# Spills moved behind the loading of x, roots between relu pairs, upper count rows computed in full

## The chip, the cores and the metric

One core of a Trainium2 chip. The metric is the device time of one execution in microseconds (us); a median of several runs is taken. Engines by the profile's names: PE (TensorE matmuls; PEld its weight loads), DVE (VectorE), ACT (ScalarE), POOL (GpSimd), SP (the engine that issues the DMAs here).

## What is computed

x is 64 x 128 x 1024 (batches, times, nodes), the weight 128 x 128, gumbel one pair for each of 1024 x 1024 node pairs.

```python
h = jnp.maximum(_layernorm(x, axis=-1), 0.0)          # over the 1024 nodes
x_avg = transpose(h, (2, 0, 1)).mean(axis=1)          # over the batches
x_norm = x_avg / jnp.maximum(norm(x_avg, axis=-1), 1e-12)
sim = (x_norm @ x_norm.T + 1.0) * 0.5
adj = (sim + gumbel0 > 1.0 - sim + gumbel1)
adj_sym = jnp.clip(adj + adj.T, 0.0, 1.0)
nmask = jnp.clip(adj_sym + jnp.eye(n), 0.0, 1.0)
common = nmask @ nmask.T
struct = where(adj_sym * (common > 1) > 0, common / common.max() * common, 0.0)
W = adj * struct;  deg = W.sum(axis=0);  Wn = dinv[:, None] * W * dinv[None, :]
out = x + transpose(einsum('sd,sbt->dbt', Wn, h @ weight) + bias)
```

## The kernel before

Batches go in 32 pairs; nodes in C = 8 blocks of 128 (KC = 4 is half of it). Each engine has its own program; semaphores tie them, and the order within an engine is the order written. All DMAs are issued by SP into one queue, in order.

**Loading x** (rounds of 8 pairs, groups of two pairs, `first(r)` on PE, ACT and DVE). SP loads a pair into one of 8 slots once the relu of the pair eight back is done (lines 301 to 309). DVE takes bn_stats (line 688) of group g and, between them, runs the small steps of group g-1: aggregate, reciprocal, one Newton step, rstd, shift (lines 633 to 672; `whole_chain` does them without bn_stats between). ACT does the square root of a group (`std`, line 452), then the relus of the group before (line 462) into 4 slots h1. POOL adds even batches (line 400), PE odd ones (line 1044). For 8 of the pairs PE multiplies h by the weight at once (`keep_product`, line 1029) and ACT copies the result to `kept` (line 482); `kept` is spilled to DRAM in 8 groups of 1 MB (line 298), one after each of the pairs 16, 20, 24 and 28 and four behind the first four gumbel loads. The last two pairs' four batches are the late ones: `late_times_weight` and `keep_late` (line 494).

**Norm and similarity.** DVE adds both sums (line 763), ACT squares (490), PE sums the columns (1059), DVE and PE form the scaled columns (1065, 772); 16 matmuls in halves give the dot products (1090). `threshold(i)` (755, DVE) and line 409 (POOL) form gumbel differences in `above`, from gumbel loads (314) of which numbers 4 to 7 wait for `s_above`. DVE compares (833) and forms sums of the first quad between.

**Graph.** PE transposes the adjacency (1101), DVE makes nmask (839, 842), ACT counts its rows (516). PE multiplies for the common neighbours (`common`, 1109): rows 0 to 2 for each k as nmask comes, rows 3 to 7 after. Only columns from the diagonal on are computed; the left part of a row is the transpose of earlier rows' right parts (`right`, ACT 535; `left`, PE 1123). ACT squares both parts (525, 529), DVE multiplies with the adjacency (857, 860) into `graph`. POOL takes the maximum over the partitions (413), then adds rows 0 to 5 (419); PE sums the columns of row 6, of that sum and of row 7 (1160). DVE and PE turn it into scaled rows (881) and DVE prepares blocks (888, 900).

**Products.** 16 quads (two pairs each) go through seven products of a two-level Strassen-like scheme (line 1237), with copies, sums and finishing on ACT, DVE and POOL. A quad's factor comes from `kept` through DRAM (360) or is made while the quad before runs: h is formed again from x (328, 505), multiplied in chunks (1177) and copied (564); `FIRST_CHUNKS` places those of quad 1. x for the result is loaded into three slots (333).

## Time and profile before

| | us |
|---|---|
| median of three runs | 977.35 (974.4 to 977.48) |
| the profiled execution | 981.56 |
| its span | 979.8 |
| busy PE, DVE, ACT, POOL | 916.6, 728.9, 353.4, 218.1 |
| granted TensorE clock, mean | 0.979 |

The profile is of one execution. A timeline row gives start, duration, engine, line, operation, tiles, count, and in brackets the idle time before and what released it. Rows with a count above one run from the first one's start to the last one's end. Durations of neighbours overlap a little. Idle time of an engine that others don't wait for costs nothing.

### The profile page before, as it was taken

What the parts mean: (1) busy time and instruction counts of PE and PEld (TensorE: products, weight loads), DVE (VectorE), ACT (ScalarE), POOL (GpSimd) and SP (SyncE); (2) the same over time, 40 slices, a digit from 0 to 9 for tenths busy, and PEclk for the clock granted to TensorE, in tenths of its full rate; (3) what the DMA queues carried; (4) which work ended last, traced back from release to release, by engine and by line L of the source; (5) the groups of instructions that cost most, each with busy time, mean ns of one, the idle gap of its engine ahead of it and who ended that gap; (6) DMA issues with size and microseconds to landing.
All of it is one profiled execution on the core that took longest, in us unless ns stands there. A gap on an engine that the chain in (4) does not pass through costs nothing.

```text
span 979.8 us, 12545 instructions
## 1 busy us (share of the span) xinstructions
PE 916.6 (94%) x4604; PEld 777.9 (79%) x4608; DVE 728.9 (74%) x1487; ACT 353.4 (36%) x566; POOL 218.1 (22%) x180
## 2 busy tenths in 40 slices
PE   1988898797899999999999999999999999999996
PEld 0555565686788888888888888888888888888885
DVE  7877767599988797886666667676767676767685
ACT  2987936242021211314242424242424242424120
POOL 2766740402111121111111111111111111111111
PEclk9999999698999999999999999999999999999999
DMA  9999990110153351714242424242424242424122
GB/s 357 333 375 360 424 362 1 44 65 1 65 193 129 130 210 49 258 65 172 86 172 87 172 86 173 86 172 87 172 85 174 77 181 72 180 72 172 44 86 87
DMA packets 36299, 149.75 MB, mean 153 GB/s; under 512 B 2832, under 2 KB 2960, under 8 KB 33168
## 3 DMA queue, kind: packets, MB, share of 16 engines
q1 hardware_dynamic: 36240, 148.97, 41.6%
q8 instruction: 36, 0.59, 0.2%
q14 instruction: 23, 0.19, 0.1%
HBM read 107.02 MB, written 41.94 MB: 152 GB/s over the span
## 4 chain that ended last, share of the span: by engine, by line
PE 80%; DVE 9%; ACT 4%; DMA 4%; issue 2%; ACTq 0%; SPq 0%; DVEq 0%
PE ps L1237 66%; PE ps L1177 7%; DMA main<-in_x 4%; ACT main L462 3%; DVE bmem L888 3%; DVE stats L688 2%; PE ps L1090 1%; PE ps L1029 1%; DVE bmem L881 1%; PE ps L1160 1%; PE ps L1109 1%; PE ps L1044 1%; ACT bmem L482 1%; DVE bmem L860 1%; DVE bmem L900 0%
## 5 line engine op out<-in xcount | busy, mean ns | idle before, releaser
L1237 PE MATMUL ps<-bmem,main 128*128 128x256 f32 x3136 | 694.3, 380 | 9.3 <-issue 4.0
L1237 PEld LDWEIGHTS ps<-bmem,main 128*128 128x128 f32 x3136 | 590.9, 191 | 88.0 <-issue 6.0
L964 DVE TENSOR_TENSOR main<-ps,main 128x512 f32<-128x512 f32 (+1 forms) x128 | 79.3, 623 | 87.9 <-PE ps L1237 87.8
L433 POOL TENSOR_TENSOR main<-main 128x256 f32<-128x256 f32 x32 | 26.1, 815 | 528.1 <-ACT main L593 528.1
L564 ACT ACTIVATE main<-ps 128x512 f32<-128x512 f32 x88 | 52.6, 597 | 211.7 <-PE ps L1177 211.7
L423 POOL TENSOR_TENSOR main<-main 128x256 f32<-128x256 f32 (+1 forms) x96 | 92.8, 994 | 135.6 <-DVE main L957 135.6
L974 DVE TENSOR_TENSOR main<-main 128x256 f32<-128x256 f32 (+1 forms) x256 | 119.4, 538 | 0.0
L1177 PEld LDWEIGHTS ps<-w_sb,main 128*128 128x128 f32 x704 | 93.1, 193 | 6.6 <-issue 1.2
L688 DVE BATCH_NORM_STATS2 stats<-main 128x6 f32<-128x512 f32 x128 | 82.0, 674 | 20.5 <-DMA main<-in_x 20.5
L1044 PE MATMUL ps<-main,ident 128*128 128x512 f32 x128 | 64.6, 639 | 34.1 <-ACT main L462 34.0
L1177 PE MATMUL ps<-w_sb,main 128*128 128x128 f32 x704 | 93.8, 277 | 1.6 <-ACT main L564 1.6
L811 DVE TENSOR_TENSOR main<-main 128x256 f32<-128x256 f32 x112 | 48.6, 434 | 54.2 <-PE ps L1237 50.9
L400 POOL TENSOR_TENSOR main<-main 128x1024 f32<-128x1024 f32 x32 | 77.3, 2417 | 45.7 <-ACT main L462 43.3
L556 ACT ACTIVATE ps<-ps 128x512 f32<-128x512 f32 x64 | 33.8, 528 | 129.7 <-PE ps L1237 129.7
L556 ACT ACTIVATE main<-ps 128x512 f32<-128x512 f32 (+1 forms) x96 | 50.5, 526 | 65.4 <-PE ps L1237 65.3
L462 ACT ACTIVATE main<-main,shift,rstd 128x1024 f32<-128x1024 f32 x64 | 74.1, 1230 | 0.0
L1044 PEld LDWEIGHTS ps<-main,ident 128*128 128x128 f32 x128 | 23.5, 200 | 61.6 <-issue 40.9
L819 DVE TENSOR_TENSOR main<-main 128x256 f32<-128x256 f32 x112 | 62.5, 558 | 3.7
L816 DVE TENSOR_TENSOR main<-main 128x256 f32<-128x256 f32 x112 | 56.8, 507 | 0.0
L813 DVE TENSOR_TENSOR main<-main 128x256 f32<-128x256 f32 x112 | 55.3, 494 | 0.0
L505 ACT ACTIVATE main<-main,shift,rstd 128x1024 f32<-128x1024 f32 x44 | 54.2, 1231 | 2.5 <-DMA main<-in_x 2.5
L1029 PEld LDWEIGHTS ps<-w_sb,main 128*128 128x128 f32 x320 | 40.4, 199 | 9.7 <-issue 9.7
(94 smaller groups left out, 545.1 us busy)
## 6 DMA issues: line engine op xcount, KB each, us to landing
main<-in_x SPq DMA_DIRECT2D x61, 1024.0 KB, 7.5
out<-main SPq DMA_DIRECT2D x32, 1024.0 KB, 4.9
main<-in_x SPq DMA_DIRECT2D x50, 512.0 KB, 5.7
spill<-bmem SPq DMA_DIRECT2D x8, 1024.0 KB, 11.8
bmem<-in_L_gnn_gumbel SPq DMA_DIRECT2D x8, 1024.0 KB, 12.8
main<-spill SPq DMA_DIRECT2D x8, 1024.0 KB, 7.3
w_sb<-in_adj SPq DMA_DIRECT2D x1, 64.0 KB, 1.8
bias_sb<-in_L_gnn_bias SPq DMA_DIRECT2D x1, 0.5 KB, 2.1
```

What stands on the lines that cost most here:

```text
L400: pool.tensor_tensor(hsum[:, :], hsum[:, :], h1[:, k % HPAIRS, 0, :], ALU.add).then_inc(s_even, 1)
L423: pool.tensor_tensor(out_, out_, in_, ALU.add).then_inc(s_pool, 1)
L462: act.activation(h1[:, k % HPAIRS, b, :], xin[:, k % XPAIRS, b, :], ACT.Relu, bias=shift[:, bass.ds(n, 1)], scale=rstd[:, bass.ds(n, 1)]). ...
L556: act.activation(to, from_, ACT.Copy).then_inc(s, 1)
L688: return dve.bn_stats(stats[:, g % 2, c // 2, 6 * f:6 * f + 6], xin[:, k, b, half(f)])
L816: dve.tensor_tensor(s2, s1, q[0, 0], ALU.subtract).then_inc(s_comb, 1)
L819: dve.tensor_tensor(s4, q[0, 1], s2, ALU.subtract).then_inc(s_comb, 1)
L964: dve.tensor_tensor(at, piece(slot, b), at, ALU.add).then_inc(s, 1)
L974: dve.tensor_tensor(out_, out_, in_, ALU.add).then_inc(s_low, 1)
L1044: last = pe.matmul(ps[:, f, :], ident[:, :], h1[:, k % HPAIRS, 1, half(f)], start=isinstance(r, int) and r == k == 0, stop=True, skip_grou ...
L1177: last = pe.matmul(ps[:, WBANK, blk(c)], hbuf[:, j % HSLOTS, blk(KC * (k % 2) + c)], w_sb[:, :], start=True, stop=True)
L1237: last = pe.matmul(piece(slot, b)[:, QUARTER * e:QUARTER * (e + 1)], left_[:, blk(c)], right_[:, c, :], start=slot in FRESH and b < 3 and ...
```

## The change

- No spill is issued during the loading of x. Behind it go gumbel 0, 1, spill 0, 1, gumbel 2, 3, spill 2, 3, then gumbel 4 to 7, then spill 4 to 7, then the h loads. Each spill has its own semaphore. The kept pairs are 0, 2, 4, 8, ... 24.
- The adjacency and nmask lie in other memory, so the loads into the result slots wait for the end of the graph.
- The square root of a group stands between the relus of the two pairs before. The last group's small steps are done for each pair; groups 13 and 14 run theirs at once.
- Sum and square of h are done in halves. threshold(3) stands behind the scaled columns. Late product 0 is in the loading loop, products 1 and 2 ahead of column sums and replication.
- Rows 0 to 3 of the common neighbours are computed in all columns; rows 4 to 7 take only their left blocks by transposition. The banks are others. DVE's sums of slot 2 stand behind the edges.
- POOL adds rows 0 to 4 before its maximum; PE sums row 5, row 6, that sum, and row 7.
- The last four chunks of quad 1 are at one place, behind product 1.

```diff
-    SPILLED = list(range(0, PAIRS - GROUP, GROUP)) + [PAIRS - GROUP - 2]
-    AHEAD = [1, 2]
+    SPILLED = [0, 2] + list(range(GROUP, PAIRS - GROUP, GROUP))
+    AHEAD = [1, 3]
...
-    FIRST_CHUNKS = (BEFORE, AFTER, AFTER, AFTER, (0, 1), (0, 3), (1, 1), (1, 3))
+    FIRST_CHUNKS = (BEFORE, AFTER, AFTER, AFTER, (1, 3), (1, 3), (1, 3), (1, 3))
...
-        adj = view(bmem, 8 * N, 4 * N).bitcast(BF16).rearrange("p (c n) -> p c n", c=C)
-        nmask = view(bmem, 12 * N, 4 * N).bitcast(BF16).rearrange("p (c n) -> p c n", c=C)
+        adj = view(main, 4 * N, 4 * N).bitcast(BF16).rearrange("p (c n) -> p c n", c=C)
+        nmask = view(main, 8 * N, 4 * N).bitcast(BF16).rearrange("p (c n) -> p c n", c=C)
...
-            return bank((0, 2, 6, 4, 2, 6, 4, 2)[i], 2)[:, c0:c1]
+            return bank((0, 2, 6, 4, 0, 2, 4, 0)[i], 2)[:, c0:c1]
+        def first_col(i):
+            return 0 if i < KC else 128 * i
+        def turned(i):
+            return ps[:, 6 + i % 2, :].bitcast(FP16)
...
-                if p >= 16 and p % GROUP == 0:
-                    spill_group((p - 16) // GROUP)
...
-            for i in range(GSLOTS):
+            for i in range(0, GSLOTS, 2):
                 load_gumbel(i)
-            for g in range(4, KEPT // 2):
-                spill_group(g)
+                load_gumbel(i + 1)
+                spill_group(i)
+                spill_group(i + 1)
             for i in range(GSLOTS, C):
                 sp.wait_ge(s_above, i - GSLOTS + 1)
                 load_gumbel(i)
+            for g in range(GSLOTS, KEPT // 2):
+                spill_group(g)
...
-            sp.wait_ge(s_sum, 1)
+            sp.wait_ge(s_sum, 2)
             for j in range(HSLOTS):
                 load_h(j)
-            load_res(0)
-            load_res(1)
-            sp.wait_ge(s_left, C - 1)
-            load_res(2)
+            sp.wait_ge(s_bits, 1)
+            for i in range(XSLOTS):
+                load_res(i)
...
-            pool.wait_ge(s_spill[0], 64)
             pool.wait_ge(s_unit, 2)
             for i in range(GSLOTS, C):
+                pool.wait_ge(s_spill[i // 2], 16)
                 pool.wait_ge(s_g[i % GSLOTS], 32)
...
-            pool.wait_ge(s_pmax, 1)
-            pool.partition_all_reduce(dmax[:, 1:2], dmax[:, 0:1], 128, RMAX).then_inc(s_gmax, 1)
-            for i in range(1, C - 2):
+            for i in range(1, C - 3):
...
+            pool.wait_ge(s_pmax, 1)
+            pool.partition_all_reduce(dmax[:, 1:2], dmax[:, 0:1], 128, RMAX).then_inc(s_gmax, 1)
...
-                    std(g, four)
                     if g or not start:
-                        for k in (2 * g - 2, 2 * g - 1):
-                            relu(k % XPAIRS, r * XPAIRS + k, four - 1)
-                    if g % 2 == 0 and (g or not start) or g == 3 and end:
-                        for b in range(2):
-                            keep(r * 2 + (g + 1) // 2 - 1, b)
+                        relu((2 * g - 2) % XPAIRS, r * XPAIRS + 2 * g - 2, four - 1)
+                    if end and g == FOURS - 1:
+                        std(g, four, 0, 2)
+                    else:
+                        std(g, four)
+                    if g or not start:
+                        relu((2 * g - 1) % XPAIRS, r * XPAIRS + 2 * g - 1, four - 1)
+                    if start and g >= 2:
+                        keep(g - 2, 0)
+                        keep(g - 2, 1)
+                    elif not start and g % 2 == 0:
+                        keep(r * 2 + g // 2, 0)
+                        keep(r * 2 + g // 2, 1)
...
-            relu(XPAIRS - 1, PAIRS - 1, PAIRS // 2 - 1)
-            act.wait_ge(s_sum, 1)
-            act.activation(wide[:, :], hsum[:, :], ACT.Square, scale=1.0 / B).then_inc(s_sq, 1)
+            std(FOURS - 1, PAIRS // 2, 2, 4)
+            relu(XPAIRS - 1, PAIRS - 1, PAIRS // 2)
+            for f in range(2):
+                act.wait_ge(s_sum, f + 1)
+                act.activation(wide[:, half(f)], hsum[:, half(f)], ACT.Square, scale=1.0 / B).then_inc(s_sq, 1)
...
-                    act.activation(right[:, RIGHT[i]:RIGHT[i + 1]], squares(i, 128 * (i + 1), N), ACT.Copy
+                    act.activation(right[:, RIGHT[i]:RIGHT[i + 1]], squares(i, 128 * FROM[i], N), ACT.Copy
                                    ).then_inc(s_right, 1)
-                if i < 2:
-                    square_right(i)
                 if i == C - 1:
                     square_left(i, 0, KC)
                     square_left(i, KC, i)
-                elif i:
+                elif i >= KC:
                     square_left(i, 0, i)
-                if i >= 2:
-                    square_right(i)
+                square_right(i)
...
-                    at_once = start and g == 1 or end and g == FOURS - 1
+                    at_once = start and g == 1 or end and g >= 2
...
                         whole_chain(g - 1, four - 1)
                         for c in range(1, 7):
-                            long_step(c)
+                            if end and g == FOURS - 1 and c == 4:
+                                dve.wait_ge(s_bn, four + 1)
+                                aggregate(g, 0, 2)
+                                long_step(c)
+                                whole_chain(g, four, 0, 2)
...
-            aggregate(LAST)
-            whole_chain(LAST, LAST)
+            aggregate(FOURS - 1, 2, 4)
+            whole_chain(FOURS - 1, LAST, 2, 4)
...
-                dve.wait_ge(s_spill[0], 64)
+                dve.wait_ge(s_spill[i // 2], 16)
...
-            for i in range(GSLOTS - 2):
-                threshold(i)
-            dve.wait_ge(s_odd, PAIRS)
+            threshold(0)
             dve.wait_ge(s_even, PAIRS)
-            dve.tensor_tensor(hsum[:, :], bank(0, 2), hsum[:, :], ALU.add).then_inc(s_sum, 1)
-            threshold(GSLOTS - 2)
-            threshold(GSLOTS - 1)
+            for f in range(2):
+                dve.wait_ge(s_last_half if f == 0 else s_odd, PAIRS if f else 1)
+                dve.tensor_tensor(hsum[:, half(f)], ps[:, f, :], hsum[:, half(f)], ALU.add).then_inc(s_sum, 1)
+            threshold(1)
+            threshold(2)
             dve.wait_ge(s_col, 1)
...
             for f in range(2):
                 dve.wait_ge(s_rep, f + 1)
                 dve.tensor_tensor(hsum[:, half(f)], ps[:, 6 + f, :], hsum[:, half(f)], ALU.mult).then_inc(s_unit, 1)
+            threshold(3)
...
-                if 2 <= i < 6:
-                    inner_sum(0, 2, i - 2)
+            inner_sums(0, 2)
...
+            for g in range(GSLOTS, KEPT // 2):
+                dve.wait_ge(s_spill[g], 16)
...
+                        if end and k == XPAIRS - 1 and f == 0:
+                            last.then_inc(s_last_half, 1)
                     last.then_inc(s_odd, 1)
-                    if k < 2:
+                    if start and k == 1:
+                        keep_product(0, 0, 0)
+                        keep_product(0, 1, 1)
+                    elif start and k in (3, 5):
+                        keep_product(k - 1, 0, k - 1)
+                        keep_product(k - 1, 1, k)
+                    elif not start and k < 2:
                         keep_product(0, k, k)
-                    elif end and k == 3:
-                        keep_product(2, 0, 2)
-                        keep_product(2, 1, 3)
-                    elif not end and k in (4, 5):
+                    elif not start and not end and k in (4, 5):
                         keep_product(4, k - 4, k - 2)
+                    elif end and k == XPAIRS - 2:
+                        pe.wait_ge(s_kept, KEPT)
+                        late_times_weight(0, 2)
...
+                    if j % KC == 0:
+                        pe.wait_ge(s_sq, j // KC + 1)
...
-            pe.wait_ge(s_kept, KEPT)
-            late_times_weight(0, 2)
-            pe.wait_ge(s_sq, 1)
+            late_times_weight(1, 4)
             column_sums(6)
-            late_times_weight(1, 4)
+            late_times_weight(2, 0)
             replicate(6, 0)
-            late_times_weight(2, 0)
-            pe.wait_ge(s_unit, 2)
             for i in range(C):
...
                 for f in range(2):
+                    if i == 0:
+                        pe.wait_ge(s_unit, f + 1)
...
-            for i in range(3, C):
-                if i == 3:
-                    pe.wait_ge(s_sym, C)
-                else:
-                    pe.wait_ge(s_edge, i - 2)
+            def full(i):
                 for k in range(C):
                     common(i, k)
-                if i == 3:
-                    left(1)
-                    left(2)
-                left(i)
-            pe.wait_ge(s_lsq, C - 2)
-            for part, source in enumerate((graph[:, C - 2, :], wide[:, :], graph[:, C - 1, :])):
-                if part == 0:
-                    pe.wait_ge(s_edge, C - 1)
-                elif part == 1:
-                    pe.wait_ge(s_colsum, C - 3)
+            pe.wait_ge(s_sym, C)
+            full(3)
+            pe.wait_ge(s_edge, 1)
+            full(4)
+            pe.wait_ge(s_edge, 2)
+            full(5)
+            left(4)
+            left(5)
+            pe.wait_ge(s_edge, 4)
+            full(6)
+            left(6)
+            pe.wait_ge(s_edge, 5)
+            full(7)
+            left(7)
+            for part, source in enumerate((graph[:, C - 3, :], graph[:, C - 2, :], wide[:, :], graph[:, C - 1, :])):
+                if part < 2:
```

## Rows read from the trace of the kernel before

**Rows 1.** The page's chain that ended last, shares of the span by line.
```profile
PE ps L1237 66%; PE ps L1177 7%; DMA main<-in_x 4%; ACT main L462 3%; DVE bmem L888 3%; DVE stats L688 2%; PE ps L1090 1%; PE ps L1029 1%; DVE bmem L881 1%; PE ps L1160 1%; PE ps L1109 1%; PE ps L1044 1%; ACT bmem L482 1%; DVE bmem L860 1%; DVE bmem L900 0%
```

**Rows 2.** Timeline of ACT, loading of x: start, us, what, count, [idle before].
```profile
32.41 0.29 ACT L452 ACTIVATE half_std<-mv,eps_sb 128x4 f32<-128x4 f32 x1
...
44.38 0.29 ACT L452 ACTIVATE half_std<-mv,eps_sb 128x4 f32<-128x4 f32 x1
...
106.54 0.30 ACT L452 ACTIVATE half_std<-mv,eps_sb 128x4 f32<-128x4 f32 x1 [1.50 <-DVE mv L635]
...
111.28 1.91 ACT L482 ACTIVATE bmem<-ps 128x1024 f32<-128x1024 f32 x2
```

**Rows 3.** Timeline of DVE, the last seven bn_stats.
```profile
107.96 4.25 DVE L688 BATCH_NORM_STATS2 stats<-main 128x6 f32<-128x512 f32 x7
```

**Rows 4.** Windows: length, busy us by engine, granted clock, DMA share, GB/s.
```profile
12.00:18.00 6.00, 0.00 (x0) 0.00 (x0) 5.86 (x15) 0.01 (x1) 0.00 (x0) 1.00 1.03 422
```

**Rows 5.** The chain in order of time, end of x to the dot products.
```profile
124.31 2.00 PE ps L1044 x4
...
128.69 1.95 PE ps L1059 x16
...
134.56 1.79 PE ps L1029 x16
136.35 13.73 PE ps L1090 x32
```

**Rows 6.** Timeline of DVE, thresholds and comparisons.
```profile
114.41 4.54 DVE L755 TENSOR_TENSOR bmem<-bmem 128x1024 f32<-128x1024 f32 x2
...
127.47 2.35 DVE L755 TENSOR_TENSOR bmem<-bmem 128x1024 f32<-128x1024 f32 x2
...
138.20 1.23 DVE L833 TENSOR_TENSOR bmem<-ps,bmem 128x1024 bf16<-128x1024 f32 x1 [2.91 <-PE ps L1090]
...
150.59 1.21 DVE L833 TENSOR_TENSOR bmem<-ps,bmem 128x1024 bf16<-128x1024 f32 x1
```

**Rows 7.** Timeline of ACT, relus of h and the last late copy.
```profile
139.92 2.50 ACT L505 ACTIVATE main<-main,shift,rstd 128x1024 f32<-128x1024 f32 x2 [2.51 <-DMA main<-in_x]
151.90 1.02 ACT L494 ACTIVATE main<-ps 128x1024 f32<-128x1024 f32 x1 [9.49 <-PE ps L1029]
```

**Rows 8.** Timeline of SP's queue, the first h loads.
```profile
130.22 2.50 SPq L328 DMA_DIRECT2D main<-in_x  x3
```

**Rows 9.** Timeline of PE, common neighbours and column sums.
```profile
153.82 1.08 PE L1109 MATMUL ps<-bmem 128*128 128x512 bf16 x5 [0.90 <-DVE bmem L842]
...
163.09 4.69 PE L1109 MATMUL ps<-bmem 128*128 128x512 bf16 x27
...
184.69 3.54 PE L1160 MATMUL ps<-ones,bmem 128*128 128x1 f32 x16 [4.84 <-DVE bmem L860]
```

**Rows 10.** Timeline of PE, first quad, behind three idle times.
```profile
226.53 14.80 PE L1237 MATMUL ps<-bmem,main 128*128 128x256 f32 x56 [4.01 <-issue]
242.41 11.49 PE L1237 MATMUL ps<-bmem,main 128*128 128x256 f32 x52 [1.08 <-DVE main L819]
256.81 7.17 PE L1237 MATMUL ps<-bmem,main 128*128 128x256 f32 x32 [2.91 <-DVE main L964]
```

**Rows 11.** Windows, the column sums (columns as in rows 4).
```profile
184.00:188.00 4.00, 3.31 (x16) 3.34 (x16) 2.10 (x5) 0.00 (x0) 3.64 (x2) 0.50 0.06 20
```

**Rows 12.** Timeline of POOL, the row sums behind the partition reduction.
```profile
175.49 2.33 POOL L419 TENSOR_TENSOR main<-bmem 128x1024 f32<-128x1024 f32 x1 [7.25 <-DVE bmem L860]
177.97 9.82 POOL L419 TENSOR_TENSOR main<-main,bmem 128x1024 f32<-128x1024 f32 x4
```

**Rows 13.** Timeline of DVE, an edge row, the end of the sums, the first scaled rows.
```profile
170.12 1.22 DVE L860 TENSOR_TENSOR bmem<-ps,bmem 128x1024 f32<-128x1024 f32 x1
...
195.17 0.23 DVE L868 TENSOR_SCALAR node<-ps,dmax 128x8 f32<-128x8 f32 x1 [9.04 <-PE ps L1160]
...
200.96 2.74 DVE L881 SCALAR_TENSOR_TENSOR bmem<-bmem,node,main 128x512 f32<-128x512 f32 x4 [1.65 <-ACT main L573]
```

More of the change, by code:

```diff
@@ L659, in set_rstd, with set_shift @@
+            def set_rstd(g, turn, b0=0, b1=4):
+                dve.wait_ge(s_newton, turn + 1)
+                _, _, std_, again, *_ = rows(g, b0, b1)
+                dve.reciprocal(rstd[:, batches(turn, b0, b1)], std_).then_inc(s_rstd, 1)
                 dve.reciprocal(again, std_).then_inc(s_rstd, 1)
[L661 to L664 removed]
+            def set_shift(g, turn, b0=0, b1=4):
+                _, _, _, again, mean, _ = rows(g, b0, b1)
+                dve.wait_ge(s_rstd, turn * 2 + 2)
+                dve.scalar_tensor_tensor(out=shift[:, batches(turn, b0, b1)], in0=mean, scalar=-1.0, in1=again,
@@ L1031, in times_weight, with late_times_weight @@
                 return last
+            def late_times_weight(n, first_bank):
+                pair = PAIRS - LATE + n // 2
+                times_weight(h1[:, pair % HPAIRS, n % 2, :], first_bank).then_inc(s_late_hw, 1)
             def first(r):
+                start = isinstance(r, int) and r == 0
                 end = isinstance(r, int) and r > 0
                 def keep_product(k, b, n):
-                    wait(pe, s_kept, r * 4 + n - 1)
+                    n = n if start else r * 4 + 2 + n
+                    wait(pe, s_kept, n - 1)
                     times_weight(h1[:, k % HPAIRS, b, :], 2 + 2 * b).then_inc(s_hw, 1)
```

115 lines of the change are left out of this document (58 added, 57 removed).

## The prediction

> **What bounds the kernel now.** I read the profile from the chain of work that ended last, then the timelines of single engines over the first 260 us, and then clock and DMA by windows. The chain gives 66% to line 1237, the matmuls of the last stage [rows 1]. Its unbroken part starts at 256.81 us [rows 10] and the change leaves its instructions alone: the same seven products for each quad, the same weighing chunks from the second quad on. So what the change is worth must arise ahead of 256.81, and each microsecond saved there is one off the end. Four stretches lie there.
>
> The loading of x runs in groups of two pairs. ScalarE's square roots mark the groups: number 3 at 32.41 us, 5 at 44.38, 14 at 106.54 [rows 2]. Up to number 5 two groups take 11.97 us. From 5 to 14, with the four spills in the queue, a group takes 62.16/9 = 6.9 us. The DMA moved 422 GB/s on x alone [rows 4], so a group of 2.1 MB could come in 5.0 us. VectorE needs eight bn_stats of 0.61 [rows 3] and some 0.6 of small steps, 5.5 us. ScalarE needs a root and four relus (4.74, from 106.54 to 111.28, of which the root is 0.2) and, every other group, two copies (1.83 net of the 1.91): 11.3 for two groups [rows 2]. The last relu ends at 124.3 [rows 5]. Then come the column norms and dot products up to 150, the graph (transposes, common neighbours, edges, column sums) up to 201, and VectorE's preparation of the seven products.
>
> **The change, part by part.** All against the profiled execution (span 979.8 us, 981.6 in all; the three runs have a median of 977.35, so I take the saving off that).
>
> *Loading x.* Spills 0 to 3 leave the middle of it. Without them the queue needs 5.0 us a group at that rate [rows 4], below ScalarE's 5.65, so ScalarE with VectorE sets the pace. The root now stands between the relus of two pairs, which closes a serial circle: relus of a pair 2.27, root 0.25, then on VectorE four bn_stats and the small steps to the shift (4 x 0.61 + 0.4 = 2.85) before the next pair's relu, 5.5 with hand-overs. In a group with copies ScalarE is busy 2.27 + 0.25 + 2.27 + 1.83 = 6.6 instead. Together 12.1 for two groups, near the 11.97 that the unspilled part shows. The third kept pair in round 0 costs 1.8, but the first pair of relus no longer waits for the root, and I come to 44.6 for root 5. Ten groups more at 6.05 put root 15 at 105.1. Behind it come, by hand, the pair before (2.3), the first pair of the last group (2.3), its second root and short chain (1.2) and its relus (2.3), with 0.8 of gaps: 114.0 instead of 124.3. **+10.3.**
>
> *Sum and norm.* PE's odd sum takes 2.0 behind that [rows 5]. Halving the sum and the square saves 1.0, but times_weight of late product 1 (1.8) now lies ahead of the column sums, which start 1.8 us behind the odd sum and not 2.4. **+0.5.** Late product 0 is moved into the loop where PE waits for relus, and product 2 now fills the wait for the norms instead of following the copies at 134.56; the dot products start right behind the replication. **+1.8** [rows 5]. Dots start at 123.7.
>
> *Thresholds.* threshold(3) now lies on VectorE between the unit columns and the first comparison. VectorE was idle for 2.91 there, waiting for the first dot [rows 6]. The operation cost 1.18 with GpSimd idle and 2.27 beside it (both pairs in [rows 6]); GpSimd starts its own four at the same moment, so I take 2.3. The first comparison comes at 126.75, 1.2 behind what the dots allow. The remaining thirteen microseconds of comparisons were VectorE's own (the last starts at 150.59), so this is kept. **-1.2.** thresholds 0 to 2 fall into waits of VectorE; spill 0 and the first gumbel have 19 us from the last x load to get there, and take three transfers of 2.5.
>
> *Loads of h behind the spills.* Here I expect a new wait. SP issues gumbel 7 only behind threshold(3), at 126.7; spills 4 to 7 follow it, and only then the h loads. At 422 GB/s [rows 4] gumbel 7, four spills and the first h (5.77 MB) take 13.7 and, with 2 of latency, h 0 lands at 142.5, h 1 at 143.8. ScalarE takes relu_of(0) and relu_of(1) before keep_late(3); in the kernel before it waited 2.51 for h, and was done by 142.4, nine microseconds early [rows 7], since SP had sent the h loads at 130.22 with only two gumbels and what was left of the spills ahead [rows 8]. Now keep_late(3) ends at 146.1. PE's first common-neighbour product needs its bank and could go at 142.3 (transposes at 140.35, plus 1.95 as from 151.87 to 153.82) [rows 9]. Queued behind the waiting relu are keep_late(3) and the eight counts; PE waits for the first. **-3.8.**
>
> The Trainium skill (DMA: Bandwidth & Descriptors, "Where 436 GB/s comes from") says that HBM to SBUF transfers are held to some 358 GB/s by the HBM side. The window of [rows 4] shows 422, so I go by the trace; by the page this wait would be 2.4 longer and the time 967.4.
>
> *Count rows in full.* Rows 1 and 2 get 128 and 256 columns more for each of eight k: 3072 columns instead of 2688, that is 0.16 each at the pace of [rows 9], **-1.4** with rounding of the waits. Row 3's extra 384 lie in the next step.
>
> *Clock.* PE is idle for most of 141.4 to 146.1. After 4.01 us idle at 226.5 it took 14.80 for 56 matmuls, which at the pace of the next 52 (11.49, so 0.221 each) would be 12.4; after 1.08 none is seen, and after 2.91 matmuls took 0.224 each [rows 10]; after 4.84 [rows 9] the granted clock is 0.50, the lower level of 1.2 GHz [rows 11]. **-2.4.** The first three count rows are done at T = 161.5 (before: 163.09 plus twelve matmuls at 0.19 = 165.35).
>
> *Edges and column sums.* Before, T to the first scaled row took 35.6 us (165.35 to 200.96) [rows 13]. Three things filled it: rows 1 to 3 went through transposes and a second square; GpSimd sat in its partition reduction until 175.49 though the second edge row was there at 171.36 (start 170.12 plus 1.22), and so began its sums 4 us late; and PE's 48 sum matmuls took 10.4 at the lower clock. Now: VectorE has 1.8 us of outer sums left at T and then edges of 1.5 each, the last at T+14, with PE's and ScalarE's work for rows 3 to 7 hidden beside them. GpSimd adds rows 0 to 4 from T+4.9 on, four at 2.43 [rows 12], until T+14.6. The reduction now follows; it has no length of its own in the trace, and 168.24 to 175.49 bounds it at 7.6 from its start. So the maximum is there at T+22.2. PE's 64 sums take 1.95 for 16 at the full clock [rows 5] and 3.54 at the lower [rows 9]: begun at T+10.9 they end at T+18.7 or T+25.1, and half and half gives T+21.9. What follows took 5.8 (195.17 to 200.96); 1.1 of it, in which PE was busy with bank filling and weighing, is now done beforehand. First scaled row at T+27.1. **+8.5.**
>
> *Preparation of the products.* VectorE's chain to 256.81 is the same. x loads into the result slots wait for the graph (3 MB, 7.5 us) and are needed 30 us later. Four weighing chunks move to one place behind slot 1; they take about 7 us of PE, before slot 2's operands exist, where PE idled for 4.01 and did three of them earlier. Zero, or 1 us lost if they stick out. The inner sums of slot 2 move behind the edges, under the wait for the maximum: zero.
>
> Sum: 10.3 + 0.5 + 1.8 - 1.2 - 3.8 - 1.4 - 2.4 + 8.5 = 12.3, so **965 us**.
>
> **The rivals.** *h arrives in time* (the queue drains sooner, or GpSimd and gumbel 7 leave more room): neither the 3.8 nor the 2.4 is lost, 959. For it: the DMA is nearly empty when gumbel 7 goes out. Against it: 5.77 MB can't come faster than at the rate seen. *The circle of root and relu is slower than its sum:* ScalarE waits for the shift with its relu in a loop where register steps run between instructions; half a microsecond exposed in each of ten groups gives 970. For it: this wait did not exist before. *PE's sums wholly at 1.2 GHz:* T+25.1 plus 5.8 instead of T+27.1, 968.8. For it: the clock stayed low through all 48 before [rows 9, 11]. *The spills were not what slowed loading,* and two groups still take 13.8: root 15 comes at 113.6, 8.5 later, 973.6, or a little more and no change. *Slower:* the root behind a relu pair makes VectorE wait for ScalarE in every group, so that 2.3 adds itself to 5.5 instead of running beside it, 8.0 a group. The last relu would end at 44.6 + 80 + 8.9 = 133.5 and the time be 984.5. It decides from 7.6 a group on, where all other gains are used up and 3 us more. Against it: VectorE has 2.2 us of other work between shift and root.
>
> **How the numbers follow.** Forecast (962 to 967.9) 0.40; h in time 0.18; slower circle 0.16; sums at the lower clock 0.14; spills not the cause 0.07, of which 0.05 is no change; slower 0.05. About 0.3% (3 us) is what a measurement of this kernel can tell from none. So faster 0.90, same 0.05, slower 0.05. Range 958 to 972: it takes in the first four cases and the DMA figure of 400 to 422.
>
> **What would show it.** Root 15 near 105 and the last relu near 114; bn_stats without waits for x; a gap of ScalarE before line 505's relus until about 142 and PE idle before the common-neighbour products, with a granted clock below 1 behind it; no gap of GpSimd before its row sums; the column sums ended by T+19 to T+25; from the first scaled row on the same 55.9 us. It is wrong if groups don't come faster than 6.5 us, or if PE has to wait in quad 0 behind the four chunks.

## The result, and the profile after

| | executions | median us | range us |
|---|---|---|---|
| kernel before | 20 | 979.25 | 974.40 to 985.08 |
| kernel changed | 20 | 973.51 | 972.06 to 975.08 |

The ratio is 0.9942 (95%: 0.9927 to 0.9957): faster, by 5.7 us where 12.3 were forecast, and outside the forecast range. The profiled executions took 981.56 us before and 973.12 after. The changed kernel also spreads over 3.0 us where the kernel before spreads over 10.7; that turned out to matter.

The chain by line is still led by the products of the last stage. They start unbroken at 247.77 us instead of 256.81 [rows 10] and then run as before: 723.6 us to the end of the span against 723.0. So what happened lies ahead of that point, as it should. The page of after, chain by line:

```profile
PE ps L1275 66%; PE ps L1215 8%; DVE bmem L911 3%; ACT main L470 2%; PE ps L1075 2%; DMA main<-in_x 2%; PE ps L1054 2%; PE ps L1142 2%; DVE stats L706 2%; PE ps L1198 1%; DVE bmem L904 1%; DVE bmem L923 0%; ACT bmem L496 0%; PE ps L1106 0%;
```

`DMA main<-in_x` had 4% before [rows 1], all of it in the loading of x. Now it has 2%, and most of that is one piece of 15.21 us from 129.98 on: the wait for h. Timeline of ScalarE of after (start, us, what, count, [idle before]), which answers to [rows 2], [rows 5] and, from 143.67 on, [rows 7]:

```profile
84.94 2.37 ACT L470 ACTIVATE main<-main,shift,rstd 128x1024 f32<-128x1024 f32 x2 [0.67 <-DVE shift L682]
87.22 0.28 ACT L460 ACTIVATE half_std<-mv,eps_sb 128x4 f32<-128x4 f32 x1
...
99.79 0.30 ACT L460 ACTIVATE half_std<-mv,eps_sb 128x4 f32<-128x4 f32 x1 [1.23 <-DVE mv L648]
...
106.33 0.29 ACT L460 ACTIVATE half_std<-mv,eps_sb 128x2 f32<-128x2 f32 x1
106.52 4.63 ACT L470 ACTIVATE main<-main,shift,rstd 128x1024 f32<-128x1024 f32 x4
...
112.45 2.37 ACT L470 ACTIVATE main<-main,shift,rstd 128x1024 f32<-128x1024 f32 x2 [1.11 <-DVE shift L682]
...
143.67 1.24 ACT L521 ACTIVATE main<-main,shift,rstd 128x1024 f32<-128x1024 f32 x1 [20.39 <-DMA main<-in_x]
145.22 1.24 ACT L521 ACTIVATE main<-main,shift,rstd 128x1024 f32<-128x1024 f32 x1 [0.31 <-DMA main<-in_x]
146.37 1.00 ACT L510 ACTIVATE main<-ps 128x1024 f32<-128x1024 f32 x1
```

Roots 87.22 and 99.79 are two groups apart: 12.6 us, and about 12.3 on average over the loading, where before it was 13.8 (44.38 to 106.54, nine groups). The last relu ends at 114.82. ScalarE then waits for h 0 until 143.67, and the last late copy, for which PE waits, ends at 147.37. SP's queue of after shows the order that does it, with [rows 8] for before:

```profile
113.83 12.63 SPq L320 DMA_DIRECT2D bmem<-in_L_gnn_gumbel  x4
126.51 2.83 SPq L306 DMA_DIRECT2D spill<-bmem  x4
129.38 2.21 SPq L337 DMA_DIRECT2D main<-in_x  x3
```

Timeline of PE of after, dot products, common neighbours, column sums, products [rows 5, 9, 10]:

```profile
124.17 14.01 PE L1123 MATMUL ps<-main 128*128 128x512 f32 x32
...
147.51 2.72 PE L1142 MATMUL ps<-main 128*128 128x512 bf16 x6 [5.92 <-ACT main L510]
...
160.82 9.35 PE L1142 MATMUL ps<-main 128*128 128x512 bf16 x44
...
174.66 4.65 PE L1198 MATMUL ps<-ones,bmem 128*128 128x1 f32 x32 [0.44 <-DVE bmem L885]
179.17 3.55 PE L1198 MATMUL ps<-ones,main 128*128 128x1 f32 x16
182.59 3.55 PE L1198 MATMUL ps<-ones,bmem 128*128 128x1 f32 x16
...
189.37 2.70 PE L1106 MATMUL ps<-main,ones 128*128 128x128 f32 x16
...
247.77 12.53 PE L1275 MATMUL ps<-bmem,main 128*128 128x256 f32 x49 [2.80 <-DVE main L989]
```

The queue while h is awaited, and the clock behind the wait: windows of after (columns as in [rows 4]; the last three are granted clock, DMA share and GB/s):

```profile
126.00:132.00 6.00, 6.00 (x15) 2.66 (x14) 5.84 (x7) 0.00 (x0) 5.92 (x3) 1.00 0.75 209
132.00:138.00 6.00, 6.00 (x15) 2.65 (x14) 6.00 (x8) 0.00 (x0) 1.89 (x1) 1.00 1.01 426
138.00:144.00 6.00, 3.02 (x33) 2.65 (x31) 4.55 (x8) 0.33 (x1) 0.00 (x0) 0.93 1.01 419
144.00:150.00 6.00, 2.49 (x6) 0.87 (x7) 0.00 (x0) 5.25 (x7) 0.00 (x0) 0.50 0.21 84
150.00:156.00 6.00, 6.00 (x39) 3.41 (x38) 2.03 (x5) 2.10 (x3) 0.00 (x0) 0.72 0.02 4
```

And the end of the graph stage on GpSimd and VectorE of after [rows 12, 13]:

```profile
168.45 2.35 POOL L424 TENSOR_TENSOR main<-bmem 128x1024 f32<-128x1024 f32 x1 [33.79 <-DVE bmem L885]
170.94 7.34 POOL L424 TENSOR_TENSOR main<-main,bmem 128x1024 f32<-128x1024 f32 x3
183.98 0.38 POOL L428 PARTITION_ALL_REDUCE dmax<-dmax  x1 [5.70 <-issue]
```
```profile
186.25 0.23 DVE L891 TENSOR_SCALAR node<-ps,dmax 128x8 f32<-128x8 f32 x1 [1.69 <-PE ps L1198]
...
191.92 2.74 DVE L904 SCALAR_TENSOR_TENSOR bmem<-bmem,node,main 128x512 f32<-128x512 f32 x4 [1.54 <-ACT main L586]
```

GpSimd begins its row sums as soon as the second edge row is there (168.45) and never waits in them; the maximum is there at 184.36. The sums of PE, not the maximum, are now what the first scaled row waits for.

Gained by each point of the profiled executions, in us (before minus after): last relu 9.4, dot products 12.0, first comparison 11.9, first common-neighbour product 6.3, T (end of the first three count rows: twelve matmuls at 0.2125 from 160.82, so 163.4) 2.0, first scaled row 9.0, unbroken products 9.0, span 8.4.

### The profile page after: what moved, and what is told of

The parts are those of the page before. It is cut to its first block, busy times and chain, and to the rows that moved or that the text cites. A ratio compares the mean times of both kernels' runs of the same rounds, so it can differ in the third digit from the quotient of the medians.

```text
span 971.4 us, 12575 instructions
## 1 busy us (share of the span) xinstructions
PE 916.9 (94%) x4618; PEld 777.7 (80%) x4618; DVE 726.9 (75%) x1494; ACT 352.0 (36%) x565; POOL 214.1 (22%) x179
## 4 chain that ended last, share of the span: by engine, by line
PE 82%; DVE 9%; ACT 3%; issue 2%; DMA 2%; SPq 0%; ACTq 0%; DVEq 0%
PE ps L1275 66%; PE ps L1215 8%; DVE bmem L911 3%; ACT main L470 2%; PE ps L1075 2%; DMA main<-in_x 2%; PE ps L1054 2%; PE ps L1142 2%; DVE stats L706 2%; PE ps L1198 1%; DVE bmem L904 1%; DVE bmem L923 0%; ACT bmem L496 0%; PE ps L1106 0%; DVE main L999 0%
## 5 line engine op out<-in xcount | busy, mean ns | idle before, releaser
L1215 PEld LDWEIGHTS ps<-w_sb,main 128*128 128x128 f32 x704 | 92.9, 193 | 9.2 <-issue 3.1
L1075 PE MATMUL ps<-main,ident 128*128 128x512 f32 x128 | 61.8, 617 | 26.9 <-ACT main L470 26.9
L1054 PEld LDWEIGHTS ps<-w_sb,main 128*128 128x128 f32 x320 | 38.3, 192 | 7.6 <-issue 7.6
```

Source lines behind the costliest of these rows:

```text
L1054: last = pe.matmul(ps[:, first_bank + c // 4, blk(c % 4)], h[:, blk(c)], w_sb[:, :], start=True, stop=True)
L1075: last = pe.matmul(ps[:, f, :], ident[:, :], h1[:, k % HPAIRS, 1, half(f)], start=start and k == 0, stop=True, skip_group_check=True)
L1215: last = pe.matmul(ps[:, WBANK, blk(c)], hbuf[:, j % HSLOTS, blk(KC * (k % 2) + c)], w_sb[:, :], start=True, stop=True)
```

## The experiments

The times of before beside them were 978.03 (23 executions), 976.70 (24) and 978.71 (17) on the three chips used (experiments 1 to 4; 5 to 8; 9 to 11); a ratio is to the one on the same chip. "After" stands for the changed kernel. Differences between medians of different chips are less sure than the ratios: before's own medians differ by 2.6 us between them (976.70 to 979.25).

### 1. h loads ahead of the last four spills

```diff
-            for g in range(GSLOTS, KEPT // 2):
-                spill_group(g)
...
             for j in range(HSLOTS):
                 load_h(j)
+            for g in range(GSLOTS, KEPT // 2):
+                spill_group(g)
```

> The changed kernel with one move: SP issues the first three h loads ahead of spills 4 to 7 instead of behind them. Theory (the h loads behind four spills cost a wait and then the clock): the trace of the changed kernel has ScalarE idle for 20.39 us before relu_of(0), PE idle for 5.92 before the first common-neighbour product, and the first two steps k at 2.5 instead of 1.3 us. With the move h 0 lands near 133, PE starts common neighbours near 142.3 instead of 147.5 at granted clock 1.00, and all later stages come 5.2 + 2.5 = 7.7 us earlier: 965.8. Rival (the clock is low there for another reason, or the wait only moves to the next engine): between 968 and 971, with the products early but slow, or with VectorE or ScalarE late instead. Rival two (the spills, now later, hold up the preparation of the products, which waits for them): no gain, 973.

Measured 965.53 (965.34 to 965.99), ratio 0.9874 (0.9841 to 0.9907). PE and ScalarE of this kernel:

```profile
143.32 1.47 PE L1141 MATMUL ps<-main 128*128 128x512 bf16 x6 [0.67 <-DVE main L866]
...
153.78 9.34 PE L1141 MATMUL ps<-main 128*128 128x512 bf16 x44
```
```profile
135.99 1.24 ACT L520 ACTIVATE main<-main,shift,rstd 128x1024 f32<-128x1024 f32 x1 [0.87 <-DMA main<-in_x]
141.75 1.02 ACT L509 ACTIVATE main<-ps 128x1024 f32<-128x1024 f32 x1 [4.52 <-PE ps L1053]
```

The late copy now waits for PE and not for h. From the last relu to the first common-neighbour product it takes 27.0 us against 32.7 in after: 5.7 is the wait. From there to T it takes 13.0 (12 x 0.2123 behind 153.78, less 143.32) against 15.9, with a granted clock of 1.00 instead of 0.50 and 0.72: 2.85 is the clock. Together they are 8.55. By the medians the time fell by 8.0; behind the last relu the profiled execution fell by 8.7 (856.6 in after, 971.4 less 114.82; 847.9 here, 964.2 less 116.34). With the clock restored, the 13.0 is 1.5 more than before's 11.5 (153.82 to 165.35): that is the price of the full rows.

### 2. Spills 0 to 3 back inside the loading

```diff
+                if p >= 16 and p % GROUP == 0:
+                    spill_group((p - 16) // GROUP)
...
-                spill_group(i)
-                spill_group(i + 1)
```

> The changed kernel with spills 0 to 3 back inside the loading of x, one after each of the pairs 16, 20, 24 and 28; all else as changed. Theory (the spills made the DMA queue the limit of loading): waits of bn_stats for x come back, the last relu ends near 123 to 124 instead of 114.7, and the time is 979 to 983, with the spread from run to run of the kernel before (974 to 985) instead of that of the changed one (972 to 975). Rival (the root between the relus brought it): the last relu stays below 118 and the time below 976.

973.62 (971.37 to 974.15), the time of after. My theory that the spills held up the loading falls. From root 5 to root 15 it takes 61.6 us, as in after (44.73 to 106.33):

```profile
47.38 0.29 ACT L460 ACTIVATE half_std<-mv,eps_sb 128x4 f32<-128x4 f32 x1
...
109.01 0.29 ACT L460 ACTIVATE half_std<-mv,eps_sb 128x2 f32<-128x2 f32 x1
```

The last relu of this execution ends at 117.51, 2.7 later than after's, but root 5 was already 2.65 late, and the first spill is issued only behind it (47.92). With the spills in the queue the DMA does more, not less; a window of this kernel, and of after at the same place:

```profile
80.00:86.00 6.00, 4.46 (x11) 1.72 (x11) 5.00 (x17) 6.00 (x8) 4.21 (x3) 1.00 1.02 417
```
```profile
80.00:86.00 6.00, 4.46 (x23) 2.94 (x23) 5.01 (x18) 5.33 (x6) 4.72 (x2) 1.00 0.85 317
```

### 3. The root ahead of both relu pairs again

```diff
-                    if g or not start:
-                        relu((2 * g - 2) % XPAIRS, r * XPAIRS + 2 * g - 2, four - 1)
...
                     if g or not start:
+                        relu((2 * g - 2) % XPAIRS, r * XPAIRS + 2 * g - 2, four - 1)
                         relu((2 * g - 1) % XPAIRS, r * XPAIRS + 2 * g - 1, four - 1)
```

> The changed kernel with the square root of a group ahead of both pairs of relus again, the last group's halves included; spills stay behind x. Theory (without spills ScalarE and VectorE pace loading whichever way the root stands, 12 us for two groups): the last relu ends within 2 us of 114.7 and the time is 973 to 976. Rival (the order of the roots is what made loading faster): the last relu near 120 and 978 or more.

975.59 (974.91 to 977.04), ratio 0.9974 (0.9952 to 0.9997), 2.1 slower than after. So the order is worth some 2 us where the spills are gone, and neither edit alone explains what was gained. In the trace these 2 us don't lie in the groups: from root 5 to root 15 they take 60.6 us (47.09 to 107.72), 1.0 less than in after. They lie in the last group, whose halves were put back too: from root 15 to the end of the last relu it takes 10.8 us instead of 8.5.

### 4. The kernel before, once more

> The kernel before, unchanged, profiled once more. The profiled execution was 981.56 us where twenty runs have a median of 979.25 and reach from 974.4 to 985.08. Theory (the spread arises while x is loaded with spills in the queue): the last relu ends at another time than 124.3 (118 to 128), and the stretch from there to the end is the same 855.5 within 1 us. Rival (it arises in the products): the last relu is at 124 and the rest differs.

One execution, 981.73, last relu at 124.24 against 124.26: the same slow loading, so the profiled execution of before was no freak. It is still 2.5 above before's median of 979.25. From there to the end it took 855.8 us, where the first profiled execution took 855.5, as the theory had it. But both lie in the same part of the spread, and its lower end stays untraced.

### 5. Root first and spills inside

The edits of 2 and 3 together.

> The changed kernel with both undone at once: the root ahead of both pairs of relus and spills 0 to 3 inside the loading. Each alone cost next to nothing (spills inside 973.6, root first 975.6, changed kernel 973.5). Theory (a circle through the load: the root of a group needs the next pair landed, the relus need that root, and they free the slot for the load four pairs on; two groups take the time to landing plus some 4.8 us, so it binds only with a full queue): the two together cost much more than the sum, a group takes 6.8 to 7.1 us again, the last relu ends near 124 and the time is 978 to 982, with a wide spread. Rival (the costs add): last relu at 121, 975 to 976. Rival two (loading was slow in the kernel before for something else that stays changed, such as the third kept pair of round 0): last relu below 120.

977.77, from 976.06 to 985.26, ratio 1.0023 (1.0003 to 1.0044). Only with both undone does the saving go, and the wide spread comes back with it (9.2 us, against 2.8 and 2.1 in experiments 2 and 3). Of the 4.2 us to experiment 2, 2.3 are the last group (10.8 us again); the rest, and the spread, is new. The profiled execution was the fastest of the twelve; its last relu ended at 119.53, not near 124, and its DMA didn't slow. Those near 985 were not traced.

### 6. The same with the aggregate taken ahead

```diff
-                        long_step(0)
                         if before:
                             dve.wait_ge(s_bn, four)
-                        long_step(1)
-                        if before:
+                            dve.reciprocal(ps[:, 7, 24:25], eps_sb[:, :])
                             aggregate(g - 1)
+                        long_step(0)
+                        long_step(1)
                         long_step(2)
```

(A small reciprocal carries the wait.) VectorE's statistics (long steps 0 and 1) stood between the data of a group and its aggregate, though they wait for the next pair's load. So the root of a group, and with it the two relu pairs behind it, waited for the load of the next pair; and that load can't be issued before the relus behind the root two groups earlier have freed its slot.

> As the kernel with root first and spills inside, and VectorE's aggregate of a group ahead of the first bn_stats of the next one (a reciprocal of a constant, 0.1 us, carries its wait), so that the root no longer needs the next pair landed. Theory (the circle through the load): two bn_stats and one pair of landing leave the circle, a group takes 6.0 to 6.3 us, the last relu ends at 117 to 120 and the time is 973 to 976.5. Rival (the bytes of the spills are the limit, or the relus' order itself): no change from the kernel without the move, 978 to 982.

975.20 (974.40 to 976.76), ratio 0.9981 (0.9962 to 0.9999): the spread is 2.4 instead of 9.2, and the median 2.6 lower, with the spills inside and the root first. That a circle through the loads (load, statistics, root, relu, slot, load four pairs on) makes the spread is supported by this. What it looks like in before is a wait of the root every other group:

```profile
79.41 0.30 ACT L452 ACTIVATE half_std<-mv,eps_sb 128x4 f32<-128x4 f32 x1 [2.58 <-DVE mv L635]
85.98 0.29 ACT L452 ACTIVATE half_std<-mv,eps_sb 128x4 f32<-128x4 f32 x1
93.50 0.30 ACT L452 ACTIVATE half_std<-mv,eps_sb 128x4 f32<-128x4 f32 x1 [2.67 <-DVE mv L635]
```

The wait is put down to VectorE, whose own wait just ahead is `DMA main<-in_x` (13.5 us in eight times from 45 to 110). In the chain that ended last, in order of time (start, us, what), three loads of before lie between relus:

```profile
44.67 2.27 ACT main L462 x2
46.96 8.77 DMA main<-in_x
...
62.29 12.81 DMA main<-in_x
...
90.85 12.43 DMA main<-in_x
```

That chain has no load between 44 and 110 us in after or in experiments 2 and 3, one in 10 (12.84) and two in 5 (9.36, 9.06). It still has two here (10.73, 10.61), so the aggregate ahead shortened the way round and didn't take the load off it. From issue to landing a load takes 10.4 us in before (median, 55 to 100 us), 11.1 in experiment 10, 9.2 here, 8.9 in 2, 8.2 in 5, 6.9 in 3 and 6.4 in after. Experiment 10 is faster than before with loads that take longer: what counts is who waits for them.

### 7. The maximum ahead of the row sums

On top of experiment 1: GpSimd's wait for `s_pmax` and its `partition_all_reduce` stand ahead of the loop of row sums, as in the kernel before.

> The kernel with the h loads ahead of the spills (965.5), and GpSimd's partition maximum ahead of its four row sums again. Theory (the maximum takes some 6 us of GpSimd, from about 158.4 to 164.6 here, and the four sums of 2.45 then end near 174.4 instead of 171.2; PE, done with rows 5 and 6 at 172.5, waits 1.9 for them): 967.2 to 967.8. Rival (the maximum takes GpSimd 0.4 us as shown, and the idle time before it is only a wait): no change or up to 2 us faster, since the maximum is there earlier. Rival two (PE's sums at 1.2 GHz are the limit and hide it): no change, 965.5.

967.92 (967.79 to 969.79), ratio 0.9908 (0.9882 to 0.9933); 2.4 more than experiment 1 by the medians, 1.9 by the spans (966.1 and 964.2), 2.3 behind the last relu (850.2 and 847.9). GpSimd and PE of this kernel:

```profile
157.88 0.38 POOL L420 PARTITION_ALL_REDUCE dmax<-dmax  x1 [22.83 <-DVE dmax L870]
165.66 2.34 POOL L426 TENSOR_TENSOR main<-bmem 128x1024 f32<-128x1024 f32 x1 [7.39 <-DVE bmem L884]
```
```profile
175.53 3.58 PE L1197 MATMUL ps<-ones,main 128*128 128x1 f32 x16 [2.44 <-POOL main L426]
```

The row sums come later and PE waits 2.44 for them. The order on GpSimd is a real part of the gain of the edge stage.

### 8. The whole count, edge and sum stage as before

On top of experiment 1: rows 0 to 3 triangular again, GpSimd with the maximum first and five row sums, PE with three sources (rows 6, sum, 7), DVE's sums of slot 2 between the edges.

> The kernel with the h loads ahead of the spills (965.5), with the whole stretch from common neighbours to column sums as in the kernel before: only columns from the diagonal on, left blocks of rows 1 to 7 by transposition, maximum first, six rows summed on GpSimd, three on PE, sums of slot 2 between the edges. Theory (that part of the change is worth what the traces show between the first common-neighbour product and the first scaled row, 47.1 us before and 41.6 here): 971.0. Rival (part of it came from the clock, and comes back with PE kept busy): 968 to 969.5.

970.87 (969.19 to 972.22), ratio 0.9928 (0.9902 to 0.9954), 5.3 more than experiment 1 (5.5 behind the last relu). PE's last two sources wait for both engines there:

```profile
171.32 3.54 PE L1196 MATMUL ps<-ones,bmem 128*128 128x1 f32 x16 [4.48 <-DVE bmem L886]
176.95 3.57 PE L1196 MATMUL ps<-ones,main 128*128 128x1 f32 x16 [2.09 <-POOL main L425]
```

Full rows and early sums are worth 5.3, the 1.5 of the longer rows already paid.

### 9. Root first, gumbels inside the loading

Experiment 3 with gumbel loads 0 to 3 at the places where before had its spills: the same bytes in the queue, read and not written.

> The kernel with the root first (975.6, spills behind x), with gumbel loads 0 to 3 inside the loading at the places where the kernel before has its spills: the same 4 MB in the queue, but reads of DRAM instead of writes. Root first with spills inside was 977.8, from 976.1 to 985.3. Theory (the spills' writes slow the loads behind them for some 5 us at a time, 260 to 300 GB/s in the kernel before, and the root first can't take that up): no such stretches, the median within 1 us of 975.6 and a spread below 3 us. Rival (4 MB more in the queue, whatever they are, make loads land too late for that order): 977 to 979 and a spread of 5 us or more.

976.90 (975.39 to 977.78), ratio 0.9976 (0.9957 to 0.9996). The spread stays at 2.4, and the median is 1.3 above experiment 3. Bytes in the queue alone didn't bring the wide spread, and the median lies just below the rival's 977. That the bytes are writes may be needed; the margin between the two theories is thin, and this isn't shown.

### 10. Before, with only the root between the relu pairs

```diff
+                    if g or not start:
+                        relu((2 * g - 2) % XPAIRS, r * XPAIRS + 2 * g - 2, four - 1)
                     std(g, four)
                     if g or not start:
-                        for k in (2 * g - 2, 2 * g - 1):
-                            relu(k % XPAIRS, r * XPAIRS + k, four - 1)
+                        relu((2 * g - 1) % XPAIRS, r * XPAIRS + 2 * g - 1, four - 1)
```

> The kernel before with one move: the root stands between the two pairs of relus; spills inside and all else as before. Theory (the order of the root is what loading needed; spills behind x add at most 1 us to that): the last relu ends at 116 to 118, the time is 972 to 974 with a spread below 3 us, so that this move alone gives what the whole change gives. Rival (the late spills and the rest of the change carry the gain): 976 or more.

970.90 (969.66 to 974.03), ratio 0.9915 (0.9883 to 0.9946). One edit of three lines does at least as much as the whole change (0.9942, 0.9927 to 0.9957; the intervals overlap). The median is below the theory's 972 and the spread of 4.4 in six executions above its 3. The profiled execution is the slowest of the six, and still its last relu ends at 116.77, 7.5 ahead of before's; behind it, it takes 855.5 us, the same as before. So in these executions the whole gain lies in the loading. Its h isn't late:

```profile
133.12 2.47 ACT L506 ACTIVATE main<-main,shift,rstd 128x1024 f32<-128x1024 f32 x2 [1.81 <-DMA main<-in_x]
```

The rest of the change doesn't pay (973.51 against 970.90). Behind the last relu after takes 856.6 us, 1.1 more than here: 2.5 gained up to the first comparison, 5.3 in the count stage and 8 to 8.7 lost by the late h come to about nothing or a small loss. Where the rest of the 2.6 lies, no trace shows. Experiment 1 has the gains without the late h, and lies 5.4 below.

### 11. Three sources for the column sums

On top of experiment 1: VectorE adds the last two graph rows, and PE sums three sources of 16 matmuls instead of four.

```diff
...
+            dve.wait_ge(s_edge, C + 1)
+            dve.tensor_tensor(last_rows, graph[:, C - 2, :], graph[:, C - 1, :], ALU.add).then_inc(s_last_rows, 1)
...
-            for part, source in enumerate((graph[:, C - 3, :], graph[:, C - 2, :], wide[:, :], graph[:, C - 1, :])):
+            for part, source in enumerate((graph[:, C - 3, :], wide[:, :], last_rows)):
...
```

> The kernel with the h loads ahead of the spills (965.5), and VectorE adds the last two graph rows (1.1 us, while it waits) so that PE sums three sources instead of four: row 5, GpSimd's sum of rows 0 to 4, and that pair. Theory (PE's 64 sum matmuls, half of them at 1.2 GHz, set the end of this stage, 179.4 against 177.3 for the maximum): the sums end at 176 to 178.3, then GpSimd's maximum binds at 177.3 to 177.5, and the time falls by 1 to 2, 963.6 to 964.6. Rival (PE idle in between loses the clock earlier, and the sums end no sooner): 965.3 or more.

964.87 (963.91 to 966.87), ratio 0.9858 (0.9825 to 0.9890). PE, GpSimd and VectorE of this kernel:

```profile
171.21 6.99 PE L1196 MATMUL ps<-ones,main 128*128 128x1 f32 x32 [1.46 <-POOL main L425]
```
```profile
177.19 0.38 POOL L429 PARTITION_ALL_REDUCE dmax<-dmax  x1 [6.03 <-issue]
```
```profile
177.60 0.16 DVE L892 RECIPROCAL dmax<-dmax 128x1 f32<-128x1 f32 x1 [3.90 <-POOL dmax L429]
178.31 0.23 DVE L894 TENSOR_SCALAR node<-ps,dmax 128x8 f32<-128x8 f32 x1 [0.55 <-PE ps L1196]
```

Sixteen matmuls less brought the end of the sums from 179.44 to 178.20, and not by 3.4: PE now waits for GpSimd (1.46), and the last 32 matmuls all run at the pace of the lower clock (0.22 each). The maximum, there at 177.6, is next. In the medians 0.7 is not more than the noise between the two kernels, so neither the theory (963.6 to 964.6) nor its rival (965.3 or more) is decided; both are faster than before and after.

## Why the prediction was wrong, point by point

Forecast 965.05, measured 973.51. The 8.46 us between them are 4.21 of anchor (981.56 less 977.35), 3.26 of terms ahead of the products (12.3 less 9.04 of measured gain), 0.6 behind them (723.6 less 723.0), which belongs to no edit I can name, and 0.39 that after's profiled execution lies below its median.

**The anchor was the largest error.** The step that failed is "so I take the saving off that", the median of the runs. The terms were read from an execution of 981.56. Of the 4.21, 1.90 is that the median of three runs lay below that of twenty (979.25), and 2.31 that the profiled execution lay above it. If long loading groups are what made that execution long, their length was taken off once in the sum and once more by the lower starting point; after, without them, scatters over 3 us only. That before's executions differ in the loading is supported and not shown: its two profiled ones and experiment 10's agree behind the last relu (855.5, 855.8 and 855.5), but none of before near 975 was traced. Off the profiled execution the same sum gives 969.3, and the range, moved with it to 962 to 976, takes in the measured time. A saving that takes away what makes executions differ can't be subtracted from the typical one. The second failure is the 3.26 of terms, above all the wait for h, forecast at 3.8 and measured at 5.7, and the edge stage, forecast at 8.5 and measured at 7.1.

**Loading x: size right, cause wrong.** Forecast +10.3, measured +9.4. Root 15 came at 106.3 (forecast 105.1), the last relu at 114.8 (114.0). Two groups took 12.3 against 12.1. The pace of ScalarE and VectorE without waits was read rightly; which edit takes the waits away was not. The sentence that without the spills "the queue needs 5.0 us a group" named them as what slowed it, and experiment 2 has them all back at no cost. The chain of before and experiments 5, 6 and 10 put in their place a circle over two groups: a root waits for the statistics of a pair that can't be loaded before the relus behind the root two groups earlier. Either edit opens it, the root between the relus (experiment 10, last relu 7.5 earlier) or the spills behind x (experiment 3). The rival "the spills were not what slowed loading" was right in its title. Its time of 973.6 meets the measured one by accident, as it had the groups no faster. The slower circle of root and relu was seen (0.67 to 1.11 idle of ScalarE ahead of a relu every other group), at a fraction of its price.

**Sum and norm, late products, threshold.** Forecast 0.5 + 1.8 - 1.2, measured 2.6 up to the dots and -0.1 behind them. threshold(3) took 1.21 (124.89 to 126.10), not the 2.3 that I took from beside GpSimd [rows 6], though GpSimd's own four began at 125.06, and the first comparison started 2.1 behind the dots as before (2.0). Of the two prices in the rows the lower was right; why GpSimd beside it cost nothing here, no run shows.

**h behind the spills.** Forecast -3.8, measured -5.7 (experiment 1). The mechanism, its place and the queue behind it came as written, and the rival "h in time" didn't. Three small things added up: h 0 landed at 143.6 and not 142.5, since the queue moved 209 GB/s from 126 to 132 us before it reached 426 and 419 in the next two windows; the copy ended at 147.4, 0.2 more behind it than forecast; and PE could have gone at 141.8 (114.82 plus the 27.0 of experiment 1), not 142.3. The clock behind it cost 2.85, forecast 2.4, and the full rows 1.5, forecast 1.4. The estimate from the Trainium skill's 358 GB/s (DMA: Bandwidth & Descriptors, "Where 436 GB/s comes from") would have put h 0 at 144.9, 1.3 late where mine was 1.1 early. The windows of this trace show 419 and 426 GB/s, so here the page's figure doesn't hold; its longer wait would have met the total (967.4) better, for a wrong reason.

**Edges and column sums.** Forecast T + 27.1 for the first scaled row, measured T + 28.5, so +7.1 instead of +8.5. PE's sums started at T + 11.3 (10.9) and ended at T + 22.7, 0.8 behind "half and half gives T+21.9": they began 0.4 later and ran a little more at the lower clock. The maximum was there at T + 21.0 (22.2). What follows the sums took 5.7, before 5.8. The step that failed here is that 1.1 of it "is now done beforehand": the change doesn't do that. Bank filling and weighing still stand behind the sums in PE's program (186.00 to 189.57), and the replication starts only behind them. Experiments 7 and 8 bear out the parts: GpSimd's order 2.4, the whole stage 5.3.

**The products.** Forecast 0, measured 0 up to 247.77: first scaled row to unbroken products took 55.85 in both, with the four chunks at one place.

Chances: faster had 0.90, and it was faster by 0.6%. The range was too narrow because all its cases started from the same wrong anchor.

## What to carry to other kernels

Take a saving off the execution whose trace gave its terms. Ask first whether the edit removes the very thing that makes executions differ; then the spread goes, and what the longest one saves isn't saved by all. A rate below the usual in a transfer queue, behind a certain transfer, doesn't name that transfer as the cause: follow one buffer slot round (load, statistics, root, relu, load again), look for the step that waits for newer data than it needs, and reorder that. And when loads are moved behind bulk writes, look up the next reader of the load that now stands last: here 4 MB of writes ahead of three loads cost 8 us of a change that without this brings 12.5 (experiment 1 against before on its chip).

## What the runs showed of the hardware, unexpected

The partition reduction is shown with 0.38 us and holds GpSimd much longer: 5.70 and 6.03 us of idle "issue" stand before it in after and in experiment 11, in before the next sum came only at 175.49 [rows 12], and in experiment 7 only at 165.66, 7.39 behind it.

In the column sums, matmuls of one column, TensorE's granted clock fell and stayed at the lower level though PE had no gap. In experiment 1 it was 1.00 up to 168 us, 0.73 from 168 to 172, and then 0.50:

```profile
172.00:176.00 4.00, 4.00 (x20) 4.00 (x20) 0.60 (x2) 0.00 (x0) 0.00 (x0) 0.50 0.00 0
176.00:180.00 4.00, 4.00 (x19) 3.56 (x19) 0.57 (x4) 0.00 (x0) 0.38 (x1) 0.50 0.00 0
```

In the loading of before the DMA's rate fell for four microseconds or so behind each spill, at a busy share of 0.9 to 1.0. Experiments 2, 5 and 6 have the same spills at the same places, and from 55 to 100 us no such stretch. The first of these windows is of before, the second of experiment 3, where no spill was in the queue:

```profile
90.00:94.00 4.00, 4.00 (x23) 2.80 (x22) 4.00 (x14) 1.33 (x3) 2.36 (x1) 1.00 0.91 280
```
```profile
80.00:86.00 6.00, 4.71 (x20) 2.45 (x19) 5.08 (x17) 6.00 (x8) 4.21 (x3) 1.00 0.90 311
```

So a rate of about 300 at a share of 0.9 doesn't need a write, and a write doesn't always bring it. What it was in before, and whether executions of before differ in it, stays open: neither profiled execution of before (981.56, 981.73) lay at the lower end of its spread.
